# C rows in three bfloat16 parts, both du on VectorE, normalisation statistics and semaphore clears moved, products added in TensorE's gaps

## The reference

```
x += tanh(g_xattn[0]) * ssm(ctx, layernorm(x))        # selective scan, 256 channels x 16 states
x += tanh(g_ffn[0])   * lora_moe(layernorm(x))        # 8 low-rank experts, top 1
x += tanh(g_xattn[1]) * attention16(layernorm(x), ctx)
x += tanh(g_ffn[1])   * bitnet_ffn(layernorm(x))
x += tanh(g_xattn[2]) * attention32(layernorm(x), ctx, positions)
x += tanh(g_ffn[2])   * moe(layernorm(x))             # 8 experts, top 2
x += tanh(g_xattn[3]) * smooth_quant(layernorm(x), w, ctx)
x += tanh(g_ffn[3])   * fp8_ffn(layernorm(x))
```

```
state = state * exp(delta_t * A[e, n]) + (delta_t * u_t) * B_t[n]
y_t   = sum over n of state * C_t[n]  + D * u_t ,  then  y * silu(layernorm(x))
```

## Time and profile before

| | |
|---|---|
| Median of three runs | 1058.19 us (1057.71 to 1058.78) |
| The profiled execution's own time | 1053.64 us |
| Its span, first to last instruction | 1051.6 us |
| TensorE busy | 886.0 us (84%) |
| VectorE busy | 727.8 us (69%) |
| ScalarE busy | 581.0 us (55%) |
| GpSimd busy | 389.6 us (37%) |
| Mean granted clock of TensorE | 0.915 |

### The profile page before, as it was taken

One profiled execution on the slowest core, in us unless ns is written; L12 is line 12 of the kernel. 1 busy time (PEld: TensorE's weight loads), 2 busy tenths in 40 slices (PEclk: granted clock), 3 DMA queues, 4 the chain that ended last, 5 costly groups with the idle time before them and its releaser, 6 DMA issues. The chain is left out here.

```text
span 1051.6 us, 16546 instructions
## 1 busy us (share of the span) xinstructions
PE 886.0 (84%) x5262; PEld 521.1 (50%) x5268; DVE 727.8 (69%) x1417; ACT 581.0 (55%) x1110; POOL 389.6 (37%) x332
## 2 busy tenths in 40 slices
PE   9488996989999999999499488998649999926587
PEld 4133333742577777776277373333425666613245
DVE  5999996788866676666778768996452234248685
ACT  6434452588677777777366365888304343205362
POOL 0566640058545555454132181000012767310232
PEclk9788888999999999999699899999859999966589
DMA  2321106500000000000000201400283332240001
GB/s 86 122 74 66 60 0 244 196 11 11 12 20 15 20 21 16 20 16 4 6 1 1 56 1 30 133 23 2 88 312 127 73 78 42 35 115 1 0 1 41
DMA packets 44283, 57.36 MB, mean 55 GB/s; under 512 B 5672, under 2 KB 35120, under 8 KB 44224
## 3 DMA queue, kind: packets, MB, share of 16 engines
q1 hardware_dynamic: 37728, 48.46, 13.9%
q0 software_dynamic: 4416, 6.03, 3.5%
q10 hardware_dynamic: 2080, 2.10, 0.6%
HBM read 50.03 MB, written 6.49 MB: 54 GB/s over the span
## 5 line engine op out<-in xcount | busy, mean ns | idle before, releaser
L1299 POOL TENSOR_TENSOR a_scratch<-a_scratch,a_inverse 128x512 f32<-128x512 f32 x64 | 66.5, 1039 | 115.1 <-DVE a_inverse L1435 115.1
L478 POOL TENSOR_TENSOR ssm_drive<-ssm_du,ssm_b_row 128x1024 f32<-128x1024 f32 x31 | 73.7, 2379 | 35.5 <-DVE ssm_state L551 35.4
L2498 PE MATMUL bank<-wup,moe_xT 128*128 x184 | 83.0, 594 | 1.2 <-issue 0.6
L438 ACT ACTIVATE bank<-ssm_delta,ssm_a_neg 128x510 f32<-128x510 f32 x64 | 44.1, 690 | 72.1 <-DVE ssm_state L551 72.1
L2292 DVE TENSOR_REDUCE a_tops<-bank 128x4 f32<-128x1024 f32 x64 | 77.7, 1223 | 8.5 <-PE bank L1974 5.5
L351 PE MATMUL bank<-ssm_seen,ident 128*128 128x512 f32 x128 | 73.4, 725 | 11.6 <-DVE ssm_seen L561 11.6
L2733 DVE TENSOR_TENSOR moe_act_f<-bank,moe_silu 128x512 f32<-128x512 f32 x23 | 15.9, 692 | 90.9 <-ACT moe_silu L2568 79.2
L2142 ACT ACTIVATE wup<-bank,a_exp_scale 128x1024 f32<-128x1024 f32 x64 | 71.1, 1113 | 13.8 <-PE bank L1997 13.8
L551 DVE TENSOR_TENSOR_SCAN ssm_state<-bank,ssm_drive 128x512 f32<-128x512 f32 x64 | 74.7, 1210 | 3.1 <-issue 0.5
L1218 ACT ACTIVATE a_scratch<-bank,a_bias,a_q_factor 128x256 f32<-128x256 f32 x128 | 71.1, 559 | 7.1 <-DVE a_bias L1422 6.8
L1030 PE MATMUL bank<-keys,a_scratch 128*128 (+1 forms) x256 | 69.1, 392 | 1.5 <-DVE xn L1362 0.7
(11 more groups left out here) (487 smaller groups left out, 2220.4 us busy)
## 6 DMA issues: line engine op xcount, KB each, us to landing
ssm_b_row<-ssm_b_spill SPq DMA_DIRECT2D x16, 512.0 KB, 3.7
wup<-in_l_up_dram SPq DMA_DIRECT2D x8, 1024.0 KB, 8.6
a_wq_in<-in_l1x_q_dram SPq DMA_DIRECT2D x32, 128.0 KB, 2.1
wdn<-in_l_down_dram SPq DMA_DIRECT2D x8, 512.0 KB, 9.7
keys<-in_l1x_o_dram SPq DMA_DIRECT2D x1, 2048.0 KB, 10.8
X<-in_x_dram SPq DMA_DIRECT2D x1, 1024.0 KB, 7.6
lora_raw<-in_l_gate_dram SPq DMA_DIRECT2D x1, 1024.0 KB, 8.1
lora_raw<-in_l_up_dram SPq DMA_DIRECT2D x1, 1024.0 KB, 10.1
```

Source lines behind the costliest of these rows:

```text
L478: pool.tensor_tensor(drive[:, k, :], du[:, k, :], b_row[:, n % NROW, :], ALU.mult).then_inc(S["drive_ready"], 1)
L1299: pool.tensor_tensor(prob[:, j, :, :], prob[:, j, :, :], inverse[:, j, :].unsqueeze(2).to_broadcast([P, 2, SEQ]), ALU.mult).then_inc(S["p_ ...
L2498: last = pe.matmul(bank[:, 2 * (i % 2) + m, :], xT[:, i % 2, c, :], wup[:, bass.ds(e, 1), c * 2 * FF + m * FF:c * 2 * FF + (m + 1) * FF] . ...
```

## The change

- The C rows. ScalarE no longer converts `select`; instead it makes `minus`, the negated identity in bfloat16. After the first two decays it copies the 32 rows from banks 2 and 3 to bfloat16 three times (`parts`, 96 rows); after each of the first two copies TensorE subtracts the copied part from the bank (`minus` times the part, accumulated), so that the next copy takes what is left. `c_rows` then multiplies a bfloat16 selection matrix of 96 rows with `parts`. The rows stand in banks 2 and 3 instead of 4 and 5, and the `select3` constant is loaded with 96 rows, behind `X`.
- `du[1]` moves from GpSimd to VectorE, behind the first drive. GpSimd's drives wait for it.
- `clear_semaphores` and its two barriers go. `clear_past` clears, on GpSimd within the next stages, what ended stages have used: in the low-rank stage behind its two memsets, at the start of the BitNet stage, and in the expert stage ahead of the fetches.
- In the tails of the second attention and of the int8 stage VectorE computes the statistics, ScalarE the root and VectorE the reciprocal of the coming normalisation (`look_ahead`, `ahead_...`). The expert stage and the last stage begin with the normalised tiles (`normalise_vector`). The table for the root is loaded ahead of the last two `bring_quad`; the last stage loads the table for silu at its start.
- In the int8 stage VectorE, not GpSimd, adds the last two tiles to `X`.
- In the int8 stage TensorE gets float32 products of 256 columns with the matrix of ones into bank 7, which nobody reads (`keep_busy`): 6 before the transposes, 8 and 14 around the spreading and 4 between the turning of the integers in round 0, 2 before the turning of the activations, then 6, 11 and 3 in round 1.

```diff
+    def clear_past(self):
+        self.nc.clear_and_free_semaphores(self.past)
+        self.past = []
...
+    def ahead_stats_of(self, dve, tiles):
+        c = self.core
+        for t in tiles:
+            dve.bn_stats(c.stats[:, t, :], c.X[:, t, :]).then_inc(self.ahead_stats, 1)
+    def ahead_aggr_of(self, dve, tiles):
+        c = self.core
+        for t in tiles:
+            dve.wait_ge(self.ahead_stats, t + 1)
+            dve.bn_aggr(c.meanvar[:, t, :], c.stats[:, t, :]).then_inc(self.ahead_aggr, 1)
+    def ahead_roots(self, act):
+        c = self.core
+        for h in range(2):
+            cols = slice(h * NT // 2, (h + 1) * NT // 2)
+            act.wait_ge(self.ahead_aggr, (h + 1) * NT // 2)
+            act.activation(c.rstd[:, cols], c.meanvar[:, cols, 1], ACT.Sqrt, bias=c.eps[:, 0:1]).then_inc(self.ahead_root, 1)
+    def ahead_reciprocal(self, dve, h):
+        cols = slice(h * NT // 2, (h + 1) * NT // 2)
+        dve.wait_ge(self.ahead_root, h + 1)
+        dve.reciprocal(self.core.rstd[:, cols], self.core.rstd[:, cols])
+    def normalise_vector(self, dve):
+        c = self.core
+        for t in range(NT):
+            dve.tensor_scalar(c.xn[:, t, :], c.X[:, t, :], c.meanvar[:, t, 0:1], c.rstd[:, t:t + 1],
+                              ALU.subtract, ALU.mult).then_inc(self.xn_ready, 1)
...
                 pe.wait_ge(S["diag_ready"], CC)
-                pe.wait_ge(S["rows_ready"], 1)
...
-                pe.wait_ge(S["select_ready"], 1)
+                pe.wait_ge(S["minus_ready"], 1)
+                for i in range(2):
+                    rows = slice(2 * NS * i, 2 * NS * (i + 1))
+                    pe.wait_ge(S["part_ready"], i + 1)
+                    pe.wait_ge(S["rows_ready"], 1)
+                    for h in range(2):
+                        last = pe.matmul(bank[0:2 * NS, 2 + h, :], minus[rows, rows], parts[rows, h * HALF:(h + 1) * HALF],
+                                         start=False, stop=True, skip_group_check=True)
+                    last.then_inc(S["part_out"], 1)
+                pe.wait_ge(S["part_ready"], 3)
+                pe.wait_ge(S["s_s"], 16)
...
-                        last = pe.matmul(bank[:, 2 + h, :], select[:, n * P:(n + 1) * P],
-                                         x_rows[:, h * HALF:(h + 1) * HALF], start=True, stop=True)
+                        last = pe.matmul(bank[:, 2 + h, :], select3[:, n * P:(n + 1) * P],
+                                         parts[:, h * HALF:(h + 1) * HALF], start=True, stop=True)
...
-                act.copy(select[:, :], select_in[:, :]).then_inc(S["select_ready"], 1)
+                act.activation(minus[:, :], core.ident[:, :], ACT.Copy, scale=-1.0).then_inc(S["minus_ready"], 1)
...
-                for m in range(STEPS):
+                decays(0)
+                for i in range(3):
+                    act.wait_ge(S["rows_done"], 1) if i == 0 else act.wait_ge(S["part_out"], i)
+                    act.copy(two(parts[2 * NS * i:2 * NS * (i + 1), :]), bank[0:2 * NS, 2:4, :]).then_inc(S["part_ready"], 1)
+                for m in range(1, STEPS):
...
-                pool.wait_ge(S["delta_ready"], CC)
-                pool.tensor_tensor(du[:, 1, :], delta[:, 1, :], u[:, 1, :], ALU.mult).then_inc(S["du_ready"], 1)
...
+                dve.wait_ge(S["delta_ready"], CC)
+                dve.tensor_tensor(du[:, 1, :], delta[:, 1, :], u[:, 1, :], ALU.mult).then_inc(S["du_ready"], 1)
...
+                    if t >= 1:
+                        dve.wait_ge(S["added"], t)
+                        s.ahead_stats_of(dve, range(t - 1, t))
+                    if t >= 2:
+                        s.ahead_aggr_of(dve, range(t - 2, t - 1))
...
+                keep_busy(6)
                 s.norm_tensor(pe)
...
+                    keep_busy((8, 6)[r])
                     spread(r, 2, diag_inv, diag_s[r], 0)
                     spread(r, 0, diag, diag_s[r], C)
+                    keep_busy((14, 11)[r])
                     for h in range(2):
                         last = turn_ints(r, x_int, xq, XB, h)
+                        if h == 0:
+                            keep_busy((4, 3)[r])
...
-                for t in range(NT):
+                for t in range(NT - 2):
                     pool.wait_ge(used[1], t + 1)
                     pool.tensor_tensor(core.X[:, t, :], core.X[:, t, :], hidden[:, t, :], ALU.add).then_inc(times, 1)
...
+                for t in range(NT - 2, NT):
+                    dve.wait_ge(used[1], t + 1)
+                    dve.tensor_tensor(core.X[:, t, :], core.X[:, t, :], hidden[:, t, :], ALU.add).then_inc(added, 1)
...
-            core.clear_semaphores()
...
-                core.clear_semaphores()
```

69 lines of the change are left out of this document (48 added, 21 removed).

## The result

| | before | after |
|---|---|---|
| Median of the runs at the result | 1057.95 us (4 runs, 1052.79 to 1058.78) | 1043.40 us (4 runs, 1042.68 to 1043.92) |
| Profiled execution, own time | 1053.64 us | 1043.92 us |
| Span, mean granted clock | 1051.6 us, 0.915 | 1042.2 us, 0.948 |
| All executions of this study beside experiments | median 1056.9, mean 1056.6 us (68 runs, 1052.7 to 1061.8) | median 1043.5, mean 1043.4 us (16 runs, 1040.4 to 1046.8) |

The ratio is 0.9869, 95% interval 0.984 to 0.9898. Against the profiled execution the sum came out: 9.7 us by its own time, where 9.1 were predicted. In part that is luck, since three profiles of the changed kernel stand at 1040.6, 1041.1 and 1043.9 us and this is the longest.

What follows compares the result with a forecast made beforehand. Each stage waits for its last engine: VectorE in the scan loop, half-speed TensorE products behind VectorE's waits in the int8 stage. Terms 1.5 + 1.8 + 1.6 + 3.75 + 0.1 + 0.3, say 9.1 us, off 1058.19 gave 1049.1 us, range 1045.5 to 1053.6.

Steps and rivals of the forecast that it cites:

- I take a gain over to it unchanged: Base of the sum: gains against the profiled 1053.64 us were carried unchanged to the median 1058.19 us, 4.55 us above the profile.
- both du: Ahead of the scan loop: with du 1 on VectorE too, 0.6 us gained, range -1.2 to 0.8.
- C rows, loop and end: First stage's scan loop: 1.5 us gained from late products mostly going, 0.6 us lost in the last gathers.
- clear before BitNet: Boundary before the BitNet stage: 2.12 to 0.30 us without the semaphore clear, 1.8 us gained, range 1.3 to 1.9.
- expert stage: Early normalisation brings tiles 3.3 us earlier, the first expert product 1.6 us, range -0.4 to 3.3.
- int8 gaps: Added products in TensorE's gaps of the int8 stage raise its clock and shorten waits: 3.75 us gained, ends 0.5 and 5.
- int8 tail: Statistics and two additions on VectorE: 5.4 to 5.6 us from rescaling to normalised tiles, 0.1 us gained, range -0.7 to 1.
- last stage: Second half of the tiles no longer waits for its root, sigmoid table loaded early: 0.3 us gained.
- Rival (c): Scan loop: lighter C products keep the clock at 1.2 GHz, TensorE bounds the loop, 1065 us, slower; chance 0.04.
- Rival (a): Expert stage: early fetches meet the expert weights and land no earlier, the 1.6 us go, 1050.7 us; chance 0.16.
- the four waits called VectorE's: Int8 stage: four of VectorE's waits were said to be for TensorE products that run at half speed.
- The turn-taking of GpSimd and VectorE: Ahead of the scan loop: du 1 on GpSimd and VectorE's first drive stretch each other to 3.25 us; alone 2.35 and 1.22.

Runs made afterwards that it cites:

- c_parts: The kernel before with the C rows in three bfloat16 parts and nothing else: 12 runs, mean 1052.6 us, ratio 0.9959 (0.9937 to 0.9982).
- after_again: The changed kernel, unchanged, run again for its spread: 1040.4 to 1046.4 us (6 runs), profiled execution 1041.13 us.
- busy_only: The kernel before with only the added unread products of the int8 stage: ratio 0.9965 (0.9946 to 0.9984), mean 3.8 us below before on the same chip.

## Why the prediction missed

The step that failed is the sentence ahead of its terms: "I take a gain over to it unchanged." The median lies 4.55 us above the profiled execution, and the one long execution of the kernel before that was profiled spends its 5.35 us in the scan loop (127.30 for 121.37 us), which is 119.05 or 119.06 us in the three profiles of the changed kernel. The term that was mis-sized by it is that of the C rows: 1.5 - 0.6 us, where the means give 4.0. Term by term, in us:

| Term | predicted | measured |
|---|---|---|
| both du | 0.6 | 1.1 (0.68 to the first product, 0.43 in step 2) |
| C rows, loop and end | 1.5 - 0.6 | 1.9 against the profile read; 7.2 to 7.8 in long executions (three profiles of six with float32 C rows over 32 rows; one between, 3.5); 4.0 on the means |
| clear before BitNet | 1.8 | 1.8 |
| expert stage | 1.6 | 1.8, all from the clear |
| int8 gaps | 3.75 | 3.8 on the means; 3.9 in the stage after, 2.0 to 4.5 over the pairs of profiles with the same tail |
| int8 tail | 0.1 | 0.06 against the profile read (5.56 to 5.50), 0.6 against kernels with the added products (6.1 to 5.5) |
| last stage | 0.3 | nothing seen (49.3 to 50.0 us before, 49.3 to 49.9 after) |

With the means where there are some, that is 4.0 + 1.1 + 1.8 + 1.8 + 3.8 + 0.6 = 13.1, and the means of all runs differ by 13.2. So close an agreement is luck: the interval of `c_parts` alone lets its 4.0 be 1.9 to 6.7, and the low-rank and BitNet stages move by 2 to 3 us on their own. A further 1.3 us of the miss is the base: three runs had a median of 1058.19, all 68 one of 1056.9.

- *C rows.* Mis-sized. I had the loop's waste from one execution and the loss at the end with the wrong sign: 0.1 us was gained there against the profile read. With the three bfloat16 parts the clock is at 1.00 at the end, while the float32 loop pays up to 2.53 us for its last gather.
- *Rival (c)* had the right mechanism on the wrong kernel. "The scan loop becomes TensorE's" when the lower level lasts several pairs: that is what the kernel before does in its long executions, and what the change removes. Its argument from a lighter load to a lower clock didn't come true: 4.31 us of work in 7.08 with a clock of 1.00.
- *Expert stage.* Right size, wrong cause. I let the tail take back what the clear gave and the statistics bring 1.6; it is the other way round. Rival (a), early fetches that land no earlier, had the mechanism: in the profile after, the last weights land at 779.35 (issued at 766.25, 13.1 us), the first fetch is issued at 775.32, and TensorE's wait for its rows ends at 779.86, 4.5 us later, where the same fetch took 3.0 us before. It didn't show in the time, because the clear gave 1.8 us.
- *Int8 stage.* Right in size and cause. The two waits named went from 1.39 and 1.26 us to 0.44 and 0.20, so the spread product is still waited for, and the clock is 0.89, just short of the 0.9 forecast. In round 0 of this profile the 1.0 us gained up to the second scale row is lost again, as that row falls to a lower clock; in `after_again` and `busy_only` it keeps its 1.02 us and the gain. One reading was wrong: of the four waits called VectorE's, show two of VectorE, one of ScalarE and one of TensorE itself, for ScalarE's copy. That last one, counted with 0.65 us, didn't shorten: 1.36 us after.
- *Int8 tail.* 5.50 us, as forecast, though its terms add up to 5.2 to 5.9 and not to 5.4 to 5.6.
- *The turn-taking of GpSimd and VectorE.* Right: 3.25 us became 1.23 once GpSimd was still. The tail's two additions suffer beside GpSimd's: 1.57 us, where I had put down 0.8 and up to 0.7 more. The Trainium skill (Advanced Engine Details and Errata, GPSIMD Details) has Pool and DVE share an interface; both rows agree with it.

## What to carry to other kernels

Before a gain is carried from a profile to a median, ask whether the profiled execution is typical: its own time against the runs is the first thing to look at, and a difference of 0.4% can be a stage that has two lengths. A stage whose engine has little slack at the lower clock is such a stage; a change that shortens that engine's work can gain more on the median than its profile shows. Products that nobody reads pay in an engine's real gaps only: look at which instruction stands behind them when the gap has gone. A transfer that is asked for earlier gains nothing if it lands into another's traffic: count the gain at its landing and not at its issue.

## What the runs showed of the hardware

- Float32 C products of the same length and number left the granted clock at 1.00 in 13 of 16 pairs with 96 rows (one execution); with 32 rows it rose and fell from pair to pair through most of the loop, most often between about 0.76 and 1.00 (six executions).
- The expert stage's first fetch took 3.3 to 4.5 us up to the product that waited for it when it was issued 2.8 to 4.0 us ahead of the landing of the last 0.5 MB load (five profiles), and landed after 2.9 to 3.0 us when it was issued 0.4 to 1.8 us ahead (five profiles). That the loads' traffic holds it up is an inference from these times.
- Stages whose work is the same take different courses on the same data: the low-rank stage 49.4 to 52.5 us, the BitNet stage 84.0 to 87.0, the float32 scan loop 121.3 to 127.3 (between two executions of one kernel: 49.4 and 51.9, 84.2 and 85.7, 121.4 and 127.3). The Trainium skill (TensorE: Matmul & The Clock Gate, Part 1: The HAM clock gate) says that the clock's watch runs on its own and isn't tied to the kernel's start, so that a kernel finds its clock rise at other points from run to run. The lengths fit that, but no run here shows the cause by itself: what decides the course at a stage's entry stays open.
